# A vision block with a mixture of experts: tokens routed tile by tile during the attention, their scatters held back to half 57, five shared products moved to the end

## The chip, the cores and the metric

The kernel runs on one core of a Trainium2 chip. The metric is the device time in microseconds (us), as a median of several runs. A profiled execution gives the rows shown below; times in it count from its first instruction. The engines are PE (TensorE), DVE (VectorE), ACT (ScalarE), POOL (GpSimd) and SP (SyncE); each works through its own instruction list in order, and semaphores tie the lists together.

## What is computed

The input x is 32 images of 3 x 112 x 112. Each is cut into 49 patches of 16 x 16, so there are 1,568 tokens of width 256. All is float32.

```python
h = patches @ W.T + b                                   # embedding
h = h + attention(layernorm(h))                         # 16 heads, causal, a difference of two softmaxes, RMS norm per head
n = layernorm(h)
gates = softmax(n @ Wg.T)                               # 16 experts
scores, inds = top_k(gates, 2); scores /= sum(scores)
y = sum over the two chosen e of score_e * (silu(n @ Wgate_e.T) * (n @ Wup_e.T)) @ Wdown_e.T      # hidden 128
shared = (silu(n @ Sgate.T) * (n @ Sup.T)) @ Sdown.T                                              # hidden 512
out = h + y + sigmoid(n @ Wsg.T) * shared
```

## The kernel before, in words

Tokens are worked on in 16 tiles of 98 (two images). Every engine's list is written out by hand from the same numbered steps. After the embedding come the **halves**: `slot(u)` on each engine holds what that engine does at half u. Halves 0 to 63 are half an image of attention each (8 heads' scores on PE, row maximum and subtraction on DVE, exponential on ACT, weighing on PE); a tile's later steps follow at fixed distances (`tile_at(u, lag)` says which tile has its step of that lag at u). For tile t POOL normalises the heads (`normalise`, `difference`, `squares`, `head_norm` at half 4t+9), takes the inverse root of the second layer norm (`h2_inverse_root`, 4t+14; it gives `rs2`) and the low part of the normalised tokens (`h2_low`, 4t+19); DVE writes the normalised tokens to `hn2x` (4t+15); PE transposes them, and multiplies by the gate weights; DVE finds the two best experts (`top2`, 4t+23). So the last tiles drain through halves 64 to 83. POOL also makes `wsh_l`, the low part of the shared expert's weights, at halves 54 to 64.

Float32 products are run as three products of split values (a high and a low part): ACT makes the high part, DVE or POOL the low one.

The **shared expert** has 16 steps v of "up" work, each with a gate and an up product on PE (`shared_product`), a silu on ACT, the product on DVE (`shared_hidden`) and the split (`shared_high` on ACT, `shared_low` on DVE). Of each four steps four token tiles can be finished: `shared_down(t)` on PE, and a DVE instruction of the same name that adds `sig * product` to h (semaphore `sh_acc`). PE's `shared_down(t)` waits for `sh_acc` to reach t-1, that is for tile t-2 to be added, as two banks alternate. Steps 0 to 4 stand in the drain; steps 5 to 15, all the downs, and the splitting of the expert weights (`split_expert`) come behind the routing.

The **routing** of all tiles stands behind the drain. DVE makes one-hot rows, PE counts with two triangular products, DVE scans them and works out for each token and choice the row of `slots_x`, a buffer in HBM that is ordered by expert and padded to blocks of 128 rows (40 blocks). POOL then issues 32 indirect DMAs (`slots_x`, line 620: 16 tiles for the first choice, then, after all have landed and a column of token numbers was rewritten, 16 for the second). The buffer has been filled with padding rows by eight DMAs on POOL during the attention (`pad_rows`).

When the scatters have landed and all shared up products are done, SP loads block after block (`bx`), and the **experts** run: PE transposes, gate and up, transpose, down; POOL scatters results to `picked`. At the **end**, pieces of `picked` are loaded (`yt`) and added with their weights by DVE, and by ACT and POOL.

## Time and profile before

| | us |
|---|---|
| median of 3 runs (419.13, 424.42, 424.2) | 424.2 |
| the profiled execution's own time | 418.47 |
| its span, first to last instruction | 416.5 |
| PE busy in the span | 350.7 (84%) |
| POOL busy | 253.7 (61%) |
| DVE busy | 272.6 (65%) |
| ACT busy | 217.3 (52%) |

The span is 2 us short of its own execution's time. A busy share is a mean over stages which have different limits, so the rows below are read stage by stage. In rows of the chain and of the timeline, the first number is the start and the second the duration, in us; "L620" is line 620 of the kernel; a bracket says how long the engine stood idle before the instruction, and what ended that.

### The profile page before, as it was taken

Reading aid. Unit: us, or ns where it says so; the run is one execution under the profiler, and the core shown is the slowest. Engines: PE = TensorE matmul, PEld = TensorE weight load, DVE = VectorE, ACT = ScalarE, POOL = GpSimd, SP = SyncE. Lnnn points to the kernel's source line nnn. Section 1 sums busy time; section 2 is a strip of 40 time slices with the busy share of each in tenths; the row PEclk is TensorE's granted clock in tenths of the full one; section 3 lists DMA queues with packets and bytes.
Section 4 is the critical chain, followed back from the end, with each engine's and each line's share of the span. In section 5 each row is a group of like instructions: output and inputs, shape, how many; then the busy total and the mean of one; then the engine's idle time right before and its main releaser. Section 6 shows DMA issues by size and latency. Waiting matters only on the chain.

```text
span 416.5 us, 10603 instructions
## 1 busy us (share of the span) xinstructions
PE 350.7 (84%) x3418; PEld 317.5 (76%) x3419; DVE 272.6 (65%) x666; ACT 217.3 (52%) x554; POOL 253.7 (61%) x432
## 2 busy tenths in 40 slices
PE   3969998999999999999989877869996988899200
PEld 3869997888888888888878777869985987789100
DVE  4588446466766667678788747966762666676275
ACT  4424435567677777777677735224431554454040
POOL 5666745046566665676567871677772466777462
PEclk9989999899999999999999999969998899999755
DMA  7622664566364545664400000983125344541194
GB/s 253 192 57 82 139 134 103 66 116 108 78 98 116 108 97 64 120 111 133 140 2 2 2 1 2 354 303 102 52 78 153 98 135 128 153 130 54 40 302 122
DMA packets 33345, 47.18 MB, mean 113 GB/s; under 512 B 4538, under 2 KB 26750, under 8 KB 32528
## 3 DMA queue, kind: packets, MB, share of 16 engines
q1 hardware_dynamic: 24670, 29.12, 29.9%
q0 software_dynamic: 4864, 11.71, 8.6%
q10 hardware_dynamic: 3762, 5.72, 4.7%
q8 instruction: 28, 0.46, 0.4%
q14 instruction: 21, 0.17, 0.2%
HBM read 23.59 MB, written 15.34 MB: 93 GB/s over the span
## 4 chain that ended last, share of the span: by engine, by line
POOL 35%; issue 23%; PE 21%; DVE 11%; DMA 6%; ACT 2%; SPq 1%; POOLq 0%; DVEq 0%
PE bank L1162 9%; POOL slots_x L620 8%; POOL on L525 4%; PE bank L1393 3%; POOL att L533 3%; DMA xr<-xt 3%; POOL x_l L494 2%; PE bank L1357 2%; POOL rs L502 2%; POOL wsh_l L596 2%; POOL ao L556 2%; PE pair L1256 2%; POOL parts L507 2%; POOL picked L640 2%; DMA yt<-picked 1%
## 5 line engine op out<-in xcount | busy, mean ns | idle before, releaser
L1256 PE MATMUL pair<-vx,PT 113*113 113x128 f32 x512 | 68.2, 276 | 1.5 <-ACT raw L764 1.5
L1256 PEld LDWEIGHTS pair<-vx,PT 113*113 113x113 f32 x512 | 60.4, 177 | 2.7 <-issue 2.0
L969 DVE TENSOR_REDUCE smax<-bank 128x8 f32<-128x392 f32 x64 | 36.0, 563 | 38.1 <-PE bank L1235 38.0
L525 POOL TENSOR_TENSOR on<-raw,rz 128x256 f32<-128x256 f32 x32 | 19.9, 621 | 60.1 <-DVE rz L1027 60.1
L640 POOL DMA_INDIRECT picked<-by,bid x40 | 39.4, 984 | 24.3 <-DVE by L1140 14.6
L1245 PE MATMUL bank<-cs,Sm 114*113 114x114 f32 x256 | 41.6, 285 | 4.9 <-DVE Sm L977 4.8
L771 ACT ACTIVATE PT<-bank 113x456 f32<-113x456 f32 x64 | 35.2, 550 | 14.3 <-PE bank L1245 13.1
L620 POOL DMA_INDIRECT slots_x<-hn2x,slot_u x32 | 33.6, 1050 | 11.9 <-issue 9.1
L1245 PEld LDWEIGHTS bank<-cs,Sm 114*113 114x113 f32 x256 | 30.2, 177 | 8.2 <-DVE Sm L977 6.3
L977 DVE TENSOR_TENSOR Sm<-bank,smax 128x392 f32<-128x392 f32 x64 | 35.8, 559 | 0.5
L1174 PE MATMUL bank<-wt_h,x_h 128*98 128x256 f32 x96 | 29.0, 302 | 7.2 <-DVE wt_l L888 6.5
L764 ACT ACTIVATE raw<-pair 64x272 f32<-64x272 f32 x64 | 24.9, 390 | 11.2 <-PE pair L1256 10.4
L838 ACT ACTIVATE bxT_h<-bank 128x256 fp32r<-128x256 f32 x40 | 15.4, 384 | 29.3 <-PE bank L1357 28.8
L1235 PEld LDWEIGHTS bank<-Ks,Qs 48*49 48x49 bf16 x1024 | 18.2, 99 | 15.9 <-issue 15.9
L1174 PE MATMUL bank<-wt_h,x_l 128*98 128x256 f32 x96 | 28.4, 296 | 0.0
L1174 PE MATMUL bank<-wt_l,x_h 128*98 128x256 f32 x96 | 28.4, 296 | 0.0
L494 POOL TENSOR_TENSOR x_l<-xr,x_h 128x588 fp32r<-128x588 f32 x16 | 23.2, 1448 | 8.1 <-ACT x_h L668 7.6
L1128 DVE TENSOR_TENSOR bxT_l<-bank,bxT_h 128x256 fp32r<-128x256 f32 x40 | 17.0, 425 | 16.2 <-ACT bxT_h L838 13.8
L1162 PE MATMUL bank<-we_h,bxT_h 128*128 x80 | 26.9, 336 | 0.0
L1235 PE MATMUL bank<-Ks,Qs 48*49 48x49 bf16 x1024 | 25.0, 185 | 0.0
L749 ACT ACTIVATE hs_h<-hs 128x392 fp32r<-128x392 f32 x16 | 8.5, 532 | 31.3 <-DVE hs L985 28.6
L1162 PE MATMUL bank<-hn2T_h,wsh_h 128*128 128x392 f32 x64 | 23.2, 362 | 1.1 <-ACT sgl L743 1.1
(188 smaller groups left out, 1111.6 us busy)
## 6 DMA issues: line engine op xcount, KB each, us to landing
slots_x<-pad POOLq DMA_DIRECT2D x8, 642.5 KB, 7.5
bx<-slots_x SPq DMA_DIRECT2D x40, 128.5 KB, 2.1
Qs<-parts SPq DMA_DIRECT2D x48, 98.0 KB
Ks<-parts SPq DMA_DIRECT2D x48, 98.0 KB
we_raw<-we SPq DMA_DIRECT2D x4, 1024.0 KB, 7.9
xr<-xt ACTq DMA_DIRECT2D x13, 294.0 KB, 3.2
we_d<-we SPq DMA_DIRECT2D x1, 2048.0 KB, 8.9
yt<-picked SPq DMA_DIRECT2D x10, 196.0 KB
```

The costliest lines, as they stand in the source:

```text
L494: G.tensor_tensor(x_l[i % 3][:], xr[i % 3][:], x_h[i % 3][:].bitcast(F32), ALU.subtract).then_inc(x_lo, 1)
L525: G.tensor_tensor(on[:].rearrange("p b m d -> p (b m) d"), raw[b][:].rearrange("p b m n -> p (b m) n")[:, :, 0:16], bc(rz[b][:].rearrange( ...
L620: G.indirect_dma_start(out=slots_x, out_offset=bass.IndirectOffsetOnAxis(ap=slot_u[:, k, i:i + 1], axis=0), in_=hn2x[:, i, :], in_offset=N ...
L640: G.indirect_dma_start(out=picked, out_offset=bass.IndirectOffsetOnAxis(ap=bid[q][:], axis=0), in_=by[q][:], in_offset=None, bounds_check= ...
L771: A.activation(PT[b][:].rearrange("p a t -> p (a t)"), bank[2 + b][0:JT, 0:4 * IC], ACT.Exp).then_inc(exped, 1)
L969: V.tensor_reduce(smax[u % 2][:], score_of(u), AX.X, ALU.max).then_inc(maxed, 1)
L977: V.tensor_tensor(Sm[b][:].rearrange("p m j s -> p (m j) s")[:, :, 0:S], score_of(u), bc(smax[b][:].unsqueeze(2), [128, 8, S]), ALU.subtra ...
L1162: last = T.matmul(out, a, b, start=(3 * m + q == 0), stop=(3 * m + q == n - 1))
L1174: last = T.matmul(bank[6 + b][0:TT, 0:D], lhs, rhs, start=(k == 0 and q == 0), stop=(k == KP - 1 and q == 2))
L1235: last = T.matmul(bank[b][SLOT * jj:SLOT * jj + S, m * S:(m + 1) * S], Qs[g % 2][r, q, n * S:(n + 1) * S], Ks[g % 2][r, q, n * S:(n + 1) * ...
L1245: last = T.transpose(bank[2 + b][0:JT, m * IC:(m + 1) * IC], Sm[b][0:IC, m].rearrange("p j s -> p (j s)")[:, 0:JT], ident[0:IC, 0:IC])
L1256: last = T.matmul(bank[4 + b][0:JT, m * 2 * VN:(m + 1) * 2 * VN].rearrange("p (j n) -> p j n", j=2), PT[b][:, m, 0:JT], vx[i % NVX][:, :, ...
```

## The change

- **Regions in place of a packed order.** `slots_x` gets one region of 1,568 + 128 rows (REG) for each expert, so a token's row is the expert's base plus the number of earlier tokens there (`run`). This is known tile by tile: DVE does `top2` at half 4t+22, `one_hot` at 4t+23, `places` at 4t+25, `slot_rows` at 4t+26; PE counts the tile with two small products at 4t+23, and ACT copies the counts at 4t+24. The packed computation behind the drain is gone; a shorter one there finds for each of the 40 blocks its row and its expert.
- **Scatters** are issued by POOL within the halves, in pairs. Tile t's first choice goes at half 57+2t, its second two halves later, in front of the next tile's first; the second waits until the first of its tile has landed, as a column is rewritten in between. `ez` (for `sig`) moves from behind the drain into POOL's half 82, `ed` (for w1, w2) into half 86, behind the scatters of these halves. The halves now go up to 89.
- **Padding**: the eight DMAs on POOL go. SP writes 128 padding rows behind each region's end when the counts are known (17 DMAs, with row numbers read from registers), and loads blocks by row numbers from registers.
- **Shared expert**: up steps 5 to 7 and downs 0 to 2 go into halves 80 to 88; behind them only steps 8 to 15 and downs 3 to 10 are left before the experts, with the splits of expert weights beginning at step 9 (before, 7), and the last one behind step 15. Downs 11 to 15 stand behind the experts (BESIDE = 11), on PE and on DVE.

The constants:

```diff
+REG = TOK + BLK
+SPARE = E * REG
-        DRAINED = 5
-        FIRST_SPLIT = 7
+        DRAINED = 8
+        FIRST_SPLIT = 9
+        BESIDE = 11
-        LAST = 4 * (NT - 1) + 24
+        LAST = 4 * (NT - 1) + 30
+        def first_at(t):
+            return 57 + 2 * t
+        FIRST_AT = {first_at(t): t for t in range(NT)}
+        SECOND_AT = {first_at(t) + 2: t for t in range(NT)}
+        DOWN_AT = {86: 0, 87: 1, 88: 2}
```

SP, behind the loads of the expert weights (`we_raw`):

```diff
+            sp.dma_start(slots_x[SPARE:SPARE + BLK, :], pad[:]).then_inc(padded, 16)
+            sp.wait_ge(prow_known, 1)
+            for e in range(E):
+                if e % BX == 0:
+                    rows_of(prow, e, 0, SPARE - BLK)
+                sp.dma_start(slots_x[bass.ds(at[e % BX], BLK), :], pad[:]).then_inc(padded, 16)
             sp.wait_ge(eids_known, 3)
             sp.wait_ge(weights_known, 2)
+            sp.wait_ge(rows_known, 1)
             sp.dma_start(we_d[:], we[:, EGU:]).then_inc(wd_in, 16)
             sp.wait_ge(sh_u, NU)
```

POOL:

```diff
+            def scatter(k, t):
+                pool.wait_ge(slot_known, t + 1)
+                pool.wait_ge(hn2_done, t + 1)
+                if k == 1:
+                    pool.wait_ge(scattered[0], 16 * (t + 1))
+                    G.tensor_copy(hn2x[:].bitcast(U32)[:, t:t + 1, D], ids[:, 1, t:t + 1]).then_inc(ids_moved, 1)
+                    pool.wait_ge(ids_moved, t + 1)
+                G.indirect_dma_start(out=slots_x, out_offset=bass.IndirectOffsetOnAxis(ap=slot_u[:, k, t:t + 1], axis=0),
+                                     in_=hn2x[:, t, :], in_offset=None).then_inc(scattered[k], 16)
...
             def slot(u):
...
+                if u in SECOND_AT:
+                    scatter(1, SECOND_AT[u])
+                if u in FIRST_AT:
+                    scatter(0, FIRST_AT[u])
+                if u == 82:
+                    pool.wait_ge(logit_done, NT)
+                    G.tensor_tensor(ez[:], inverse_euler[:], logits[:, :, E], ALU.pow).then_inc(e_exp, 1)
+                if u == 86:
+                    pool.wait_ge(gate_diff, 1)
+                    G.tensor_tensor(ed[:], euler[:], dl[:], ALU.pow).then_inc(e_exp, 1)
                 if 54 <= u < 54 + 2 * NS and u % 2 == 0:
```

ACT, in `slot(u)`:

```diff
+                if (t := tile_at(u, 24)) is not None:
+                    act.wait_ge(counted, t + 1)
+                    act.wait_ge(run_done, t + 1)
+                    A.activation(ahead[:].rearrange("p a e -> p (a e)"), bank[7][0:TT, E + 1:3 * E + 1], ACT.Copy).then_inc(counts_kept, 1)
```

DVE, with its steps of `slot(u)` (`one_hot` stands first in a half, `places` and `slot_rows` near its end):

```diff
+            def one_hot(t):
+                dve.wait_ge(topped, 2 * t + 2)
+                V.tensor_copy(ixf[:], ix8[:, t, 0:TOPK]).then_inc(place_step, 1)
+                dve.wait_ge(place_step, 5 * t + 1)
+                V.tensor_tensor(oh[:], bc(iota.unsqueeze(1), [TT, TOPK, E]), bc(ixf[:].unsqueeze(2), [TT, TOPK, E]), ALU.is_equal).then_inc(place_step, 1)
+                dve.wait_ge(place_step, 5 * t + 2)
+                need(dve, counted, t)
+                V.tensor_tensor(both[:], oh[:, 0], oh[:, 1], ALU.add).then_inc(both_done, 1)
+
+            def places(t):
+                dve.wait_ge(counts_kept, t + 1)
+                dve.wait_ge(run_done, t + 1)
+                V.tensor_tensor(place[:], ahead[:, 0], run[:], ALU.add).then_inc(place_step, 1)
+                dve.wait_ge(place_step, 5 * t + 3)
+                V.tensor_tensor(chosen_at[:], oh[:], bc(place[:].unsqueeze(1), [TT, TOPK, E]), ALU.mult).then_inc(place_step, 1)
+
+            def slot_rows(t):
+                V.tensor_tensor(run[:], ahead[:, 1], run[:], ALU.add).then_inc(run_done, 1)
+                dve.wait_ge(place_step, 5 * t + 4)
+                V.tensor_reduce(slotr[:], chosen_at[:], AX.X, ALU.add).then_inc(place_step, 1)
+                dve.wait_ge(place_step, 5 * t + 5)
+                V.tensor_copy(slot_u[:, :, t], slotr[:]).then_inc(slot_known, 1)
...
+                if u == 86:
+                    dve.wait_ge(e_exp, 1)
+                    V.tensor_scalar(ez1[:], ez[:], 1.0, None, ALU.add).then_inc(routing, 1)
+                    dve.wait_ge(routing, 1)
+                    V.reciprocal(sig[:], ez1[:]).then_inc(weights_known, 1)
+                    dve.wait_ge(weights_known, 1)
+                if u - 1 in DOWN_AT:
+                    shared_down(DOWN_AT[u - 1])
```

DVE, behind the halves and still ahead of step 8 (this wait was there before, too, ahead of step 6):

```diff
             dve.wait_ge(e_exp, 2)
             link(V.tensor_scalar(ed1[:], ed[:], 1.0, None, ALU.add))
```

PE, in `slot(u)`, then in its table of up steps, then behind the experts:

```diff
+                if u in DOWN_AT:
+                    shared_down(DOWN_AT[u])
...
+            SHARED_AT = {66: (0, 0), 67: (0, 1), 69: (1, 0), 70: (1, 1), 71: (2, 0), 72: (2, 1), 73: (3, 0), 75: (3, 1), 76: (4, 0), 79: (4, 1),
+                         80: (5, 0), 81: (5, 1), 82: (6, 0), 83: (6, 1), 84: (7, 0), 85: (7, 1)}
...
+            pe.wait_ge(b_hT, NBLK)
+            for t in range(BESIDE, NT):
+                shared_down(t)
```

## Rows read from the trace of the kernel before

**Rows 1.** The chain that ended last, from the second scatters to the experts
```profile
293.64 0.96 POOL slots_x L620
...
314.07 2.53 DMA slots_x<-hn2x,slot_u
...
316.66 2.04 DMA bx<-slots_x
...
318.84 1.21 PE bank L1357 x4
```

**Rows 2.** Timeline of PE: a down's first product, an up step's, the next down's
```profile
302.97 0.28 PE L1162 MATMUL pair<-wsh_h,hs_h 128*98 128x256 f32 x1
...
304.38 0.34 PE L1162 MATMUL bank<-hn2T_h,wsh_h 128*128 128x392 f32 x1
...
306.55 0.28 PE L1162 MATMUL pair<-wsh_h,hs_h 128*98 128x256 f32 x1
```

**Rows 3.** Busy time by stretch: start:end length, PE, PEld, DVE, ACT, POOL, granted clock, DMA
```profile
220.99:250.12 29.13, 24.72 (x269) 21.46 (x267) 19.05 (x51) 18.26 (x47) 23.14 (x50) 1.00 0.01 2
...
100.00:200.00 100.00, 96.82 (x1273) 84.46 (x1272) 71.39 (x190) 70.66 (x181) 63.87 (x136) 1.00 0.55 110
270.00:280.00 10.00, 6.85 (x31) 6.56 (x30) 7.36 (x20) 2.77 (x5) 7.56 (x9) 0.72 0.91 314
```

**Rows 4.** Timeline of DVE: the tokens' write at half 39, a small routing step
```profile
176.53 0.75 DVE L1016 TENSOR_SCALAR hn2x<-h,mv,rs 98x256 f32<-98x256 f32 x1 [1.04 <-POOL rs L564]
...
264.26 0.17 DVE L1071 TENSOR_SCALAR cnts<-cnt 98x16 int32<-98x16 int32 x1
```

**Rows 5.** Timeline of POOL: its five waits in halves 57 to 71
```profile
223.06 0.62 POOL L525 TENSOR_TENSOR on<-raw,rz 128x256 f32<-128x256 f32 x1 [0.26 <-DVE rz L1027]
...
228.75 0.62 POOL L525 TENSOR_TENSOR on<-raw,rz 128x256 f32<-128x256 f32 x1 [1.29 <-DVE rz L1027]
...
233.15 0.62 POOL L525 TENSOR_TENSOR on<-raw,rz 128x256 f32<-128x256 f32 x1 [0.25 <-DVE rz L1027]
...
238.41 0.62 POOL L525 TENSOR_TENSOR on<-raw,rz 128x256 f32<-128x256 f32 x1 [0.92 <-DVE rz L1027]
...
247.00 0.21 POOL L546 TENSOR_TENSOR nt<-r 128x16 f32<-128x16 f32 x1 [1.31 <-ACT r L786]
```

**Rows 6.** The scatters by line: nanoseconds of one; landing, all and those at 262-275
```profile
L620 POOL DMA_INDIRECT slots_x<-hn2x,slot_u x32: 942/949/1965, 269.2 to 314.1; - x32
...
DMA to landing us min/median/max: 2.5/2.7/8.0
...
DMA to landing us min/median/max: 3.1/4.0/8.0
```

**Rows 7.** Timeline of POOL: a power of 98x16, a one-column copy of token numbers
```profile
260.94 2.91 POOL L608 TENSOR_TENSOR ed<-euler,dl 98x16 f32<-98x16 f32 x1 [0.55 <-DVE dl L1057]
...
318.83 0.18 POOL L629 COPY bid<-bx 128x1 uint32<-128x1 uint32 x1 [3.82 <-DMA bx<-slots_x]
```

**Rows 8.** Timeline of PE: a down after a wait, and the next down
```profile
275.26 0.50 PE L1162 MATMUL pair<-wsh_h,hs_h 128*98 128x256 f32 x1 [3.15 <-DVE h L1115]
...
281.59 0.28 PE L1162 MATMUL pair<-wsh_h,hs_h 128*98 128x256 f32 x1
```

**Rows 9.** Timeline of DVE: a split of expert weights, and two steps' shared hidden
```profile
284.77 1.23 DVE L1107 TENSOR_TENSOR we_l<-we_raw,we_h 128x1024 fp32r<-128x1024 f32 x1 [0.38 <-ACT we_h L826]
...
304.50 0.56 DVE L985 TENSOR_TENSOR hs<-sgl,bank 128x392 f32<-128x392 f32 x1
...
308.14 0.55 DVE L985 TENSOR_TENSOR hs<-sgl,bank 128x392 f32<-128x392 f32 x1
```

**Rows 10.** Timeline of POOL: the scatter issued beside that split
```profile
284.87 1.95 POOL L620 DMA_INDIRECT slots_x<-hn2x,slot_u  x1 [0.30 <-issue]
```

**Rows 11.** Timeline of PE's last instruction, and of DVE's first addition of results
```profile
387.56 1.22 PE L1393 MATMUL bank<-we_d,bhT 128*128 x4
...
397.25 0.49 DVE L1150 SCALAR_TENSOR_TENSOR h<-yt,w,h 98x256 f32<-98x256 f32 x1 [8.00 <-DMA yt<-picked]
```

More of the change, by code:

```diff
@@ L141, in build @@
         woff = keep("woff", [1, NBLK // BX + 1, 2 * BX], I32)
+        pad = keep("pad", [128, ROW])
+        ixf = keep("ixf", [TT, TOPK])
+        oh = keep("oh", [TT, TOPK, E], BF16)
+        both = keep("both", [TT, E], BF16)
+        ahead = keep("ahead", [TT, 2, E])
+        place = keep("place", [TT, E])
+        chosen_at = keep("chosen_at", [TT, TOPK, E])
+        slotr = keep("slotr", [TT, TOPK])
+        run = keep("run", [TT, E])
+        prow = keep("prow", [1, E], I32)
+        rows = keep("rows", [1, NBLK], I32)
         one_bf = keep("one_bf", [128, 128], BF16)
@@ L234, in build @@
         hs_l = [la(f"hs_l{n}", [128, SB, SH], F32R) for n in range(2)]
+        ya = Zone(late.at, ceiling).take
         we_h = la("we_h", [128, EGU], F32R)
@@ L270, in build @@
         bid = [ba(f"bid{n}", [BLK, 1], U32) for n in range(BX)]
-        ya = Zone(shared.at, ceiling).take
         yt = [ya(f"yt{n}", [TT, TOPK, YG, D]) for n in range(NT // YG)]
@@ L445, in _, with rows_of @@
                 sp.dma_start(we_raw[:, cols], we[:, cols]).then_inc(we_in[n], 16)
+            regs = [SP.alloc_register(f"row{n}") for n in range(BX)]
+            at = [None] * BX
+            def rows_of(table, n0, low, high):
+                SP.load(regs, table[0:1, n0:n0 + BX])
+                for n in range(BX):
+                    at[n] = SP.snap(regs[n], min_val=low, max_val=high)
             def load_block(b):
+                if b % BX == 0:
+                    rows_of(rows, b, 0, SPARE)
                 if b >= BX:
@@ L1047, in _ @@
                 slot(u)
-            dve.wait_ge(topped, 2 * NT)
-            done = [0]
+            done = [1]
             def link(ins):
@@ L1064, in _ @@
[L1064 to L1070 removed]
+            dve.wait_ge(run_done, NT + 1)
@@ L1272, in slot @@
                     need(pe, logit_done, t)
+                    need(pe, counts_kept, t - 1)
                     for k in range(KD):
@@ L1287, in slot @@
                     end.then_inc(gated, 1)
+                if (t := tile_at(u, 23)) is not None:
+                    pe.wait_ge(both_done, t + 1)
+                    pe.wait_ge(logit_done, t + 1)
+                    T.matmul(bank[7][0:TT, E + 1:2 * E + 1], up_bf[0:TT, 0:TT], both[:], start=True, stop=True)
+                    T.matmul(bank[7][0:TT, 2 * E + 1:3 * E + 1], one_bf[0:TT, 0:TT], both[:], start=True, stop=True).then_inc(counted, 1)
                 if 0 <= u - 2 < HALVES:
@@ L1336, in shared_down @@
                                                      for b in range(SB)]).then_inc(sh_y, 1)
-            for v in range(DRAINED, NU + DOWN_LAG):
-                if v < NU:
-                    shared_product(v, 0)
-                    shared_product(v, 1)
+            for i in range(NT + 1):
+                step(i)
+            slot(0)
+            for i in range(NT + 1, NT + 4):
+                step(i)
+            for u in range(1, LAST):
+                slot(u)
+            for v in range(DRAINED, NU):
+                shared_product(v, 0)
+                shared_product(v, 1)
                 shared_down(v - DOWN_LAG)
```

227 lines of the change are left out of this document (93 added, 134 removed).

## The prediction

> **What bounds the kernel now.** I read the chain first. From the last scatters it runs straight into the experts: the last indirect DMA starts at 314.07 and lands 2.53 later, a block is loaded in 2.04, and the experts' first product starts at 318.84 [rows 1]. The reader is to see that scatters pace this stretch: from 293.64 to 314.07 fifteen steps take 20.4, so 1.36 each. But they are not alone. PE's timeline [rows 2] shows the shared expert beside them: a down takes 1.41 (302.97 to 304.38), an up step 2.17 (304.38 to 306.55). Step 15 ends at 306.55, and six downs more carry PE nearly to the landing of the scatters. So two paths end within a microsecond of each other, and a change has to shorten both. In the attention PE is busy 96.8 of 100 us [rows 3]: it sets the pace there. Last I read POOL from half 57 on, since the change puts its scatters there: between 220.99 (start of half 57) and 250.12 (end of half 71) its waits are only 0.26, 1.29, 0.25, 0.92 and 1.31 [rows 5]. It has 4.03 us to spare in 29.13, so 25.1 of its own work (23.1 by busy time alone [rows 3]; the rest is gaps between dependent steps). That is the finding on which the forecast rests.
>
> **Ahead of half 57.** Nine tiles are routed: eight small DVE instructions each, at 0.17 [rows 4] and some gap, say 1.6 us; two small PE products, one ACT copy. Most of the DVE work falls into waits like the 1.04 ahead of the tokens' write [rows 4]; what doesn't, and PE's own two products, I take as 0.2 to 0.25 a tile, an estimate, since PE has only 3.2% to spare: 2 us, with 0 (all hidden) and 4 (a quarter of DVE's 1.6 x 9 = 14.4) as ends. POOL's eight padding DMAs go, which gives nothing where PE sets the pace. So half 57 starts on POOL at 223.0.
>
> **POOL from half 57 to half 71.** Added are first scatters of tiles 0 to 7 and second ones of 0 to 6: 15 x 1.36 = 20.4. Seven copies of token numbers at 0.18 [rows 7] with a gap make 1.8. Their landing waits are hidden by other work here. 25.1 + 20.4 + 1.8 = 47.3, against 29.1 before: POOL ends half 71 at 270.3 instead of 250.1. This doesn't stay on POOL. DVE's write of the normalised tokens waits for POOL's root and stands ahead of the subtraction that PE's transposes need, so the last attention halves are held too; and `wsh_l` in half 64, which PE's first shared product needs, comes some 9 us later. The ends: 23.1 of own work and the median of 0.95 [rows 6] with a gap of 0.3 take off 2.0 and 1.7.
>
> At one place a rule of the Trainium skill can be weighed. A scatter that began at 284.87, a tenth after a DVE split of two SBUF operands at 284.77, took 1.95 instead of 0.95 [rows 9, 10]. The Trainium skill (SBUF — State Buffer, section "SBUF: two separate sides") says that DVE and GpSimd share a port pair under an exclusive lock, and that GpSimd cannot write a DMA's descriptors while DVE holds it; the trace agrees at this place. By the rule, were each of the 25 scatters up to `ez` held by 1.0 as this one was, the sum would be 25 higher, beyond the last rival below. The 1.36 used here is a mean that holds such cases as often as they came.
>
> **From half 73 on** POOL has little else to do, and the pair itself is a chain: the second scatter of a tile waits for the landing of its first. Landing 2.53, copy 0.2, gap 0.3, and the second's pitch of 1.3 make 4.3 a tile. Tile 7's first starts at about 269.0, tile 11's therefore at 286.2. In half 74 lies the last root, near 274.5, and in half 79 the last `h2_low`, near 283; what is left of POOL's own work fits into the landing waits. `h2_low` releases the loads of the expert weights, so the next landing competes with 4 MB: I take 4.0, the median of the five beside those loads, not 2.53; the ends are 2.5 and 8.0 [rows 6]. Tile 12's first then starts at 292.0 and ends at 293.0, and `ez`, moved behind it, ends 2.9 later [rows 7]: 295.9.
>
> **What waits for `ez`.** DVE stands in half 86 at `sig`; queued behind it are the hidden product of step 7 and the down of tile 0. PE has by then done steps 0 to 7 and downs 0 and 1 (tile 15's gate product comes near 277; behind it are seven single products of half of 2.17 and two downs, 10.4, and some waits: about 289) and stands at down 2, which needs the down of tile 0 on DVE. Two small DVE steps, the hidden product and the down (0.25 + 0.2 + 0.55 + 0.5) put PE's start at 297.4. Left on PE up to the end of step 15 are eight downs, 11.3, and eight up steps, 17.4: 326.1. After the only such wait before (3.15) the granted clock of that stretch was 0.72, a mixture of 1.2 and 2.4 GHz, and a down and an up step took 6.33 (275.26 to 281.59) instead of 3.58 [rows 2, 3, 8]; here PE idles for 8, so I add 2.8 (ends 0 and 2.8): step 15 ends at 328.9, against 306.55.
>
> `ed`, behind the pair of half 85, ends near 307; DVE waits for it ahead of the hidden product of step 8, which PE needs for the up half of step 10, at about the same time. I cost that at 0, with 2 as upper end.
>
> **From step 15 to the experts.** Of the six downs that stood here one is left, so the five moved ones give 7.0. But the splits now begin two steps later and the last stands behind step 15. DVE starts a step's hidden product 1.6 after PE ended it (308.14 against 306.55), its round takes 3.64, and the last split 1.23 more [rows 2, 9]: the experts, which need all splits, start 6.5 after step 15, at 335.4, against 318.84. That is +16.6. Scatters don't end last: after `ed` two tiles are left, landed near 316. The padding on SP, 17 small DMAs, stands in front of the load of the down weights, but that load waits for `ed` as well; it has from 307 to PE's 328.9 to land.
>
> **The experts and the end.** Per block nothing changes; row numbers in registers are read eight at a time, ahead of loads with eight blocks' lead: 0, or up to 2. Downs 11 to 15 take 7.0 on PE after 388.78, and DVE's part 0.6, while the first results arrive 8.5 after PE's end [rows 11]: 0. If PE ran them at the lower clock they would take twice that, and the end would be 5 later.
>
> **Sum.** 418.47 + 16.6 = 435.1 on the profiled execution's footing, of which attention is 2.0, landing beside the loads 1.5, and the clock 2.8. The profiled time lies with the lowest of the three runs, 5.7 under their median; on the median's footing it is 440.8. I name 437, between them. With all low ends (2.0, 2.0, 1.7, 1.5, 2.8) 6.6 is left, with the high ones (2 + 4 + 2 + 2 + 5 more) about 32.
>
> **Rivals.**
> - *POOL has room after all (faster).* If gaps and landings cost nothing, POOL's time to `ez` is 23.1, 2 more of late own work, 25 x 0.95 = 23.8 and 2.9, from 220.99: 272.8. Then PE is released at 274.3, ends step 15 at 303.0, and the experts start at 309.5: 9.3 less, 409 to 415. It gains where `ez` ends before 282. For it: the landing lies beside other work in most halves. Against it: the scatters stood 1.36 apart where POOL did nothing else, not 0.95 [rows 1, 6], and the landing is awaited by name. Chance 0.06.
> - *The same sum with the low ends (no difference that can be measured, about 2% here).* Attention hides the routing, the landings stay at 2.5, the clock holds: +3 to +8.5, 422 to 433. For it: almost no transfers in halves 57 to 71 (2 GB/s) [rows 3]. Against it: all ends would have to fall low. Chance 0.22.
> - *The forecast*, +9 to +20: 427 to 444. Chance 0.58.
> - *Landings of 8 beside the loads, for two or three tiles*, so that `ed` too holds DVE and PE, or downs at the end that show: +21 to +32, 440 to 455. The 8.0 speaks for it, the median of 2.7 against it [rows 6]. Chance 0.14.
>
> The change may also fail of its aim at one point only, the moved downs, if they lengthen the end: that is the 5 in the high ends. Eight in ten: I leave out the gain and most of the last case, 424 to 446. Faster by over 2%: 0.06; within: 0.22; slower: 0.72.
>
> **What the profile after would show.** POOL without waits between halves 57 and 71, ending there near 270; landing as what ends POOL's waits from half 73 on; `ez` near 296; PE idle for several us ahead of down 2, released by DVE's h; step 15 ending near 329, the experts starting 6 to 7 later, behind a DVE split and not behind a block's load; the end unchanged. I am wrong if scatters beside the attention are shorter than 0.95, if POOL still waits in halves 57 to 66, or if PE's down 2 doesn't wait.

## The result, and the profile after

Slower, by more than the range allowed: 457.79 us as a median of four runs (451.95 to 462.99), against 421.66 for the kernel before on the same chip; ratio 1.077, 95% interval 1.058 to 1.097. Forecast were 437.0 and 424 to 446. Medians in this document are over all runs of a kernel, while ratios and intervals compare only the executions without the slower state that both kernels sometimes fall into (for the changed kernel 451.95 and 456.51). The profiled execution of the changed kernel is its slowest run (462.99; span 461.1; mean granted clock 0.902, for the kernel before 0.944), so its rows say more about places than about the median. Two more profiles of the unaltered kernel, below, repeat what is read here.

The chain that ended last, in order of time (start, duration, what); it answers to [rows 1]:

```profile
360.31 0.96 ACT we_h L862
361.27 0.02 issue
361.29 1.23 DVE we_l L1167
362.52 0.39 DVE h L1031
362.91 1.14 DVE we_l L1167
364.05 0.04 issue
364.10 0.70 PE bank L1414 x2
```

Not a scatter and not a block's load leads into the experts now, but the splits of the expert weights, as forecast. The experts start at 364.10 instead of 318.84: 45.3 later.

POOL's timeline: half 57's first row, the last row of half 71, then the rows up to `ed` ([rows 5, 7]):

```profile
245.97 0.22 POOL L580 TENSOR_TENSOR nt<-r 128x16 f32<-128x16 f32 x1
...
292.36 0.95 POOL L613 DMA_INDIRECT slots_x<-hn2x,slot_u  x1 [0.30 <-issue]
...
311.26 0.96 POOL L613 DMA_INDIRECT slots_x<-hn2x,slot_u  x1 [0.30 <-issue]
317.31 0.18 POOL L611 COPY hn2x<-ids 98x1 uint32<-98x1 uint32 x1 [5.10 <-DMA slots_x<-hn2x,slot_u]
...
320.31 2.96 POOL L636 TENSOR_TENSOR ez<-inverse_euler,logits 98x16 f32<-98x16 f32 x1
...
331.03 3.55 POOL L639 TENSOR_TENSOR ed<-euler,dl 98x16 f32<-98x16 f32 x1
```

From 245.97 to 293.31 halves 57 to 71 take 47.3, the very sum that was forecast. But they begin at 245.97, 25.0 later than before, where 2 were forecast. Behind them `ez` ends 30.0 later (forecast 25.6); POOL's longest wait for a landing on the way is 5.10, behind the first scatter of tile 11 (311.26).

The scatters by line ([rows 6]), and `both`, the sum of the two one-hot rows (ns, least, median, most), each as the view of its line or tile gives it:

```profile
L613 POOL DMA_INDIRECT slots_x<-hn2x,slot_u x32: 952/973/1802, 248.2 to 343.4; - x32
...
DMA to landing us min/median/max: 2.5/2.6/6.3
```

```profile
L1052 DVE TENSOR_TENSOR both<-oh x16: 166/978/2282, 135.8 to 306.8; 98x16 bf16<-98x16 bf16 x16
```

DVE's timeline in the attention, `ez`, the hidden products of steps 8 and 15, the last down, and the first result ([rows 4, 9, 11]):

```profile
179.55 1.08 DVE L1052 TENSOR_TENSOR both<-oh 98x16 bf16<-98x16 bf16 x1
180.56 0.55 DVE L1006 TENSOR_REDUCE smax<-bank 128x8 f32<-128x392 f32 x1
...
323.31 0.17 DVE L1118 TENSOR_SCALAR ez<-ez 98x16 f32<-98x16 f32 x1 [9.19 <-POOL ez L636]
...
335.32 0.56 DVE L1022 TENSOR_TENSOR hs<-sgl,bank 128x392 f32<-128x392 f32 x1
...
359.19 0.55 DVE L1022 TENSOR_TENSOR hs<-sgl,bank 128x392 f32<-128x392 f32 x1
...
440.98 0.48 DVE L1031 SCALAR_TENSOR_TENSOR h<-pair,sig,h 98x256 f32<-98x256 f32 x1 [0.92 <-PE pair L1217]
443.53 0.48 DVE L1205 SCALAR_TENSOR_TENSOR h<-yt,w,h 98x256 f32<-98x256 f32 x1 [2.08 <-DMA yt<-picked]
```

PE's timeline at half 22, at a counting product, at down 2, at the first product of down 10 (it follows step 15), and at the experts ([rows 2, 8]):

```profile
136.59 2.05 PE L1311 MATMUL pair<-vx,PT 113*113 113x128 f32 x8 [2.70 <-issue]
...
180.69 0.21 PE L1347 MATMUL bank<-both,up_bf 98*98 98x16 bf16 x1 [1.24 <-DVE both L1052]
...
324.91 0.50 PE L1217 MATMUL pair<-wsh_h,hs_h 128*98 128x256 f32 x1 [7.93 <-DVE h L1031]
...
355.80 0.32 PE L1217 MATMUL pair<-wsh_h,hs_h 128*98 128x256 f32 x1
...
364.10 1.11 PE L1414 MATMUL bank<-cs,bx 128*128 128x128 f32 x4 [6.68 <-DVE we_l L1167]
```

Three rows speak of the attention. `both` adds 16 numbers per partition and takes 1.08, and 2.28 at most, where the small step of before took 0.17 [rows 4]; PE's counting product waits 1.24 for it; and once, at half 22, PE stands 2.70 with nothing to wait for that the profile shows. The other rows were forecast: the wait for `ez` (7.93; forecast 8) and the splits that release the experts. PE stands 6.68 for these, but only behind down 10; from the end of step 15 (355.80, where down 10 starts) to the experts it is 8.3, where 6.5 were forecast. The moved downs are over on DVE at 441.46, before the first result at 443.53: they are hidden.

By stretch, in attention (start:end length, PE, PEld, DVE, ACT, POOL, granted clock, DMA), as [rows 3]:

```profile
151.00:163.00 12.00, 10.75 (x116) 9.48 (x115) 9.04 (x27) 6.90 (x20) 6.31 (x14) 0.86 0.35 39
163.00:175.00 12.00, 10.77 (x140) 9.40 (x139) 9.76 (x30) 7.86 (x22) 5.61 (x13) 1.00 0.34 44
```

PE's busy time falls from 96.8% to just under 90%, and in the first of the two its granted clock is 0.86, a mixture of 1.2 and 2.4 GHz, where before it was 1.00 throughout [rows 3].

So from profile to profile (spans 416.5 and 461.1): 25.0 ahead of half 57, 18.2 in halves 57 to 71 (forecast 18.2), 2.1 from there to the experts (forecast 3.6 less), 0.7 less behind them. Of the 25.0, 3.8 are there at half 1 already (its row maximum at 80.76 instead of 76.93); other kernels of the new form have 75.20 to 85.07 there, so that part is not shown to be the change's.

### The profile page after: what moved, and what is told of

Same layout as the page of the kernel before. It is cut to its first block, busy times and chain, and to the rows that moved or that the text cites. A ratio compares the mean times of both kernels' runs of the same rounds, so it can differ in the third digit from the quotient of the medians.

```text
span 461.1 us, 11109 instructions
## 1 busy us (share of the span) xinstructions
PE 373.6 (81%) x3448; PEld 338.0 (73%) x3449; DVE 299.2 (65%) x788; ACT 219.3 (48%) x570; POOL 250.1 (54%) x439
## 4 chain that ended last, share of the span: by engine, by line
PE 31%; issue 18%; POOL 17%; DVE 14%; DMA 10%; SPq 6%; ACT 2%; POOLq 0%; DVEq 0%; ACTq 0%
PE bank L1217 10%; PE pair L1311 7%; SPq L447 5%; DMA slots_x<-hn2x,slot_u 4%; PE bank L1300 4%; PE bank L1450 3%; POOL slots_x L613 3%; PE bank L1290 3%; DMA xr<-xt 2%; PE bank L1414 2%; DMA Ks<-parts 2%; POOL wsh_l L644 2%; DVE both L1052 2%; DMA yt<-picked 2%; ACT we_h L862 2%
## 5 line engine op out<-in xcount | busy, mean ns | idle before, releaser
L1311 PE MATMUL pair<-vx,PT 113*113 113x128 f32 x512 | 74.8, 293 | 3.0 <-issue 2.7
L1311 PEld LDWEIGHTS pair<-vx,PT 113*113 113x113 f32 x512 | 66.5, 193 | 4.4 <-issue 3.3
L671 POOL DMA_INDIRECT picked<-by,bid x40 | 39.2, 981 | 26.6 <-DVE by L1193 16.9
L1300 PE MATMUL bank<-cs,Sm 114*113 114x114 f32 x256 | 44.5, 300 | 2.6 <-DVE Sm L1014 2.6
L1300 PEld LDWEIGHTS bank<-cs,Sm 114*113 114x113 f32 x256 | 32.4, 189 | 5.2 <-DVE Sm L1014 3.0
L1290 PEld LDWEIGHTS bank<-Ks,Qs 48*49 48x49 bf16 x1024 | 19.2, 103 | 17.1 <-issue 17.1
L1217 PE MATMUL bank<-hn2T_h,wsh_h 128*128 128x392 f32 x64 | 25.3, 396 | 3.0 <-POOL wsh_l L644 2.5
L1414 PE MATMUL bank<-cs,bx 128*128 128x128 f32 x80 | 16.6, 294 | 12.3 <-DVE we_l L1167 6.7
L1290 PE MATMUL bank<-Ks,Qs 48*49 48x49 bf16 x1024 | 26.1, 188 | 0.0
```

Source lines behind the costliest of these rows:

```text
L671: G.indirect_dma_start(out=picked, out_offset=bass.IndirectOffsetOnAxis(ap=bid[q][:], axis=0), in_=by[q][:], in_offset=None, bounds_check= ...
L1217: last = T.matmul(out, a, b, start=(3 * m + q == 0), stop=(3 * m + q == n - 1))
L1290: last = T.matmul(bank[b][SLOT * jj:SLOT * jj + S, m * S:(m + 1) * S], Qs[g % 2][r, q, n * S:(n + 1) * S], Ks[g % 2][r, q, n * S:(n + 1) * ...
L1300: last = T.transpose(bank[2 + b][0:JT, m * IC:(m + 1) * IC], Sm[b][0:IC, m].rearrange("p j s -> p (j s)")[:, 0:JT], ident[0:IC, 0:IC])
L1311: last = T.matmul(bank[4 + b][0:JT, m * 2 * VN:(m + 1) * 2 * VN].rearrange("p (j n) -> p j n", j=2), PT[b][:, m, 0:JT], vx[i % NVX][:, :, ...
L1414: last = T.transpose(bank[par][:, k * BLK:(k + 1) * BLK], bx[q][:, k * 128:(k + 1) * 128], ident)
```

## The experiments

My theory after reading the trace: the routing beside the attention costs what came in ahead of half 57, most of it by `both`, which POOL's work holds up on DVE. The rival: it is something else of the new program (the embedding, its code, the scatters and their landings). Each expectation says what either would give.

For every profile I read three stage lengths from DVE's row maxima and PE's first expert product. They say where a change of the time lies. Each is from one execution, so the clock of that execution is in it:

| kernel | median us (runs) | half 22 to 26 | half 26 to 57 | half 57 to experts |
|---|---|---|---|---|
| before | 420.5 to 424.9 (four medians) | 10.88 | 79.52 | 99.16 |
| changed | 457.79 (4) | 17.62 | 95.29 | 118.01 |
| again | 458.70 (4) | 16.61 | 92.89 | 119.21 |
| both_reduced | 445.20 (4) | 17.55 | 82.77 | 119.24 |
| counts_late | 452.49 (4) | 16.27 | 88.22 | 118.97 |
| scatters_behind | 459.79 (4) | 17.51 | 95.80 | 119.30 |
| late_routing | 442.32 (4) | 16.21 | 78.69 | 120.15 |
| spread | 440.87 (4) | 18.08 | 96.05 | 99.19 |
| ez_early | 459.44 (4) | 17.96 | 95.49 | 119.92 |
| spread_all | 430.66 (4) | 16.54 | 85.58 | 101.21 |
| pads | 457.32 (4) | 10.90 | 94.33 | 119.42 |
| downs_ahead | 460.34 (4) | 18.15 | 92.86 | 124.63 |
| best | 419.08 (5) | 14.73 | 88.39 | 94.61 |
| best_pads | 427.29 (4) | 10.90 | 90.26 | 92.24 |
| pads_2 | 456.24 (6) | 10.90 | 98.16 | 118.31 |
| again_2 | 457.07 (6) | 13.30 | 92.90 | 119.13 |
| ez_ed_early | 446.93 (6) | 16.61 | 95.69 | 108.00 |
| best_second | 414.09 (6) | 12.40 | 82.30 | 91.41 |

Runs of one kernel lie up to 15 apart here, so a difference of 2 between two medians says nothing.

### The attention ahead of half 57

**again** is the changed kernel, unaltered. 

> The changed kernel once more, unaltered, for a second profile. In the first one half 57 starts on POOL at 245.97 instead of 220.99, 25 later, where 2 was forecast; 3.8 of it stand already at half 1, and 6.7 come between halves 22 and 26, around one stall of PE of 2.70 for which nothing is shown. Theory A (the routing steps beside the attention hold DVE and PE, some 1.2 to 2.1 a tile): about 15 to 18 of the 25 come again, the 3.8 and the 6.7 may not. Theory C (the profiled execution was disturbed as a whole): under 8 come again. Time by A 450 to 458, by C under 445.

 Measured 458.70, just above theory A's range. POOL's half 57 starts at 242.88, so 21.9 of the 25 come again: 3.7 of them are there at half 1 (80.61), and the stall of 2.70 at half 22 is there too. Theory C fell.

**both_reduced** takes the sum from one operand:

```diff
-                V.tensor_tensor(both[:], oh[:, 0], oh[:, 1], ALU.add).then_inc(both_done, 1)
+                with nc.allow_low_precision(reason="zeros and ones"):
+                    V.tensor_reduce(both[:], oh[:].rearrange("p k e -> p e k"), AX.X, ALU.add).then_inc(both_done, 1)
```

> One DVE instruction altered: the sum of the two one-hot rows is a reduction over one operand instead of an addition of two. Theory A (that addition of two SBUF operands is held by POOL's instruction, 1.08 instead of 0.17, and PE stands 1.24 behind it in front of its counts): the instruction falls to 0.2, PE's wait to under 0.5, and the time by 0.8 x 10 tiles, some 8 us, against the changed kernel. Theory B (it is the number of DVE's instructions in front of the row maximum that delays, not the hold): the time falls by under 2 us. Also possible under A: the hold moves to the next instruction of two operands, then under 4 us.

 Measured 445.20, 12.6 less than the changed kernel's first median and 13.5 less than again. The same tile's view:

```profile
L1053 DVE TENSOR_REDUCE both<-oh x16: 185/186/189, 131.9 to 290.5; 98x16 bf16<-98x32 bf16 x16
```

0.19 each time, and half 26 to 57 falls by 10.1 against again. Some of the 10.1 is PE's clock: it was granted 1.00 there and 0.96 in again. So most of the routing's price in that stage is one instruction of 16 elements per partition, with what it does to the clock. How it comes to 1.08 can be read from POOL beside it, in the changed kernel:

```profile
179.42 0.55 POOL L598 TENSOR_TENSOR rs<-ve,half_neg 98x1 f32<-98x1 f32 x1
179.94 0.61 POOL L575 TENSOR_TENSOR sq<-att 128x256 f32<-128x256 f32 x1
180.51 0.56 POOL L603 TENSOR_TENSOR hn2T_l<-h2T,hn2T_h 128x196 fp32r<-128x196 f32 x1
```

`both`, with two operands in SBUF, is listed from 179.55 to 180.63 and ends 0.08 behind POOL's `sq` (180.55); in each of the eight tiles from 154 to 238 of this trace it ends 0.06 to 0.09 behind `sq`. Near the end, where nothing of POOL's or only a scatter lies beside it, it takes 0.17. With one operand it takes 0.19 beside the same work. The row maximum of the half, which PE needs, stands behind it. The Trainium skill (SBUF — State Buffer, section "SBUF: two separate sides") has this as an exclusive lock between a DVE operation on two SBUF operands and a GpSimd operation that reads SBUF, for a whole instruction. The two forms, 1.08 and 0.19, agree with it; but the trace shows `both` held over two instructions of POOL's, the end of `rs` and all of `sq`, and over three where it takes 2.28. In the kernel before it was the tokens' write that ended behind POOL's `sq` (0.75 [rows 4]; 0.96 as a mean of nine from 135 to 235). In the changed kernel it starts later and takes 0.40, as `both` has taken the wait.

**counts_late** puts PE's two count products behind the weighing of their half:

```diff
+                if 0 <= u - 2 < HALVES:
+                    weigh(u - 2)
                 if (t := tile_at(u, 23)) is not None:
                     pe.wait_ge(both_done, t + 1)
...
-                if 0 <= u - 2 < HALVES:
-                    weigh(u - 2)
```

> PE's two count products stand behind the weighing of the same half instead of ahead of it; DVE is left as it is. Theory A: PE's wait of 1.24 a tile is covered by the 1.05 of the weighing, 5 to 10 us less than the changed kernel, in the attention alone. Theory B (DVE's row maximum and subtraction come late, and the next half's transposes wait for them): PE's wait only moves to the transposes, 0 to 3 us less.

 Measured 452.49, 6 less than again; half 26 to 57 falls by 4.7. That is theory A, at the low end of its range. What a wait costs is thus also a matter of what is queued behind it.

**late_routing** routes only tiles 9 to 15: each `tile_at` at lags 23 to 26 becomes `routed`, and the semaphores count from tile 9. It leaves out the expert results of tiles 0 to 8.

```diff
+        N0 = 9
+
+        def routed(u, lag):
+
+            t = tile_at(u, lag)
+            return t if t is not None and t >= N0 else None
```

> This kernel leaves out the routing of tiles 0 to 8 (one-hot rows, counts, places): their tokens go to fixed rows that no block reads, and the last additions take other tiles' results; scatters keep their number and places. Theory A (the routing beside the attention is what came in ahead of half 57): POOL's half 57 begins near 222 to 228 in place of 242 to 246, the stall of 2.4 to 2.7 on PE at half 23 is gone or stands at half 59 now, where the first count products are, and the time is 434 to 442. Rival B (something else of the new program slows the attention, such as the embedding or the layout of its code): half 57 begins at 236 or later, and the time stays above 450.

 Measured 442.32, at the upper end of theory A's range; POOL's half 57 starts at 225.33 (222 to 228 expected). Half 26 to 57 takes 78.69, as before (79.52): so all of the 13 to 16 there is the routing. The theory stands, with one exception:

```profile
132.62 2.05 PE L1319 MATMUL pair<-vx,PT 113*113 113x128 f32 x8 [2.42 <-issue]
```

The stall at half 22 is still there, with no tile routed yet. There the theory fell.

**pads** and **pads_2** put the eight padding DMAs of before back on POOL, into a buffer that nobody reads:

```diff
+                if u % 6 == 5 and u // 6 < NT // 2:
+                    pad_rows(u // 6)
```

> The changed kernel with the eight padding DMAs of the kernel before put back on POOL at their old halves, into a buffer that nothing reads; nothing else differs. Theory C (PE stands 2.4 to 2.7 at half 22 in every kernel of the new form, with the routing of tiles 0 to 8 or without it, because its instructions arrive later when the padding DMAs don't lie beside the stacking loads; 5.5 to 6.7 with the low clock behind it): the stall is gone, half 22 to half 26 takes 10.9 again, and the time is 451 to 454. Rival (the stall is due to something else, as where the code lies): it stays at 2.4 to 2.7, and eight DMA instructions of 0.83 on POOL leave the time at 457 to 462.

 Measured 457.32. The stall is gone in all three runs with these DMAs (pads, pads_2, best_pads): half 22 to 26 takes 10.90 in each. It is there, 1.62 to 2.70, in each of the fourteen other profiles of the new form. Queues in one microsecond (packets, MB, share), first late_routing from 129 to 130, then the kernel before from 126 to 127:

```profile
q1 hardware_dynamic: 84, 0.06, 51.7%
q8 instruction: 1, 0.02, 10.3%
```

```profile
q0 software_dynamic: 30, 0.10, 26.4%
q1 hardware_dynamic: 81, 0.06, 19.3%
q8 instruction: 1, 0.02, 6.3%
```

A packet of instructions (16 KB, the ninth of 28 in queue q8) starts 2.9 ahead of half 22 in the kernel before (row maximum at 129.28), and only 0.1 ahead of it in late_routing (129.48); PE stands from 130.2 to 132.6. The same holds in every profile: with the padding DMAs the ninth packet starts 2.2 to 2.9 ahead of half 22, without them from 1.4 ahead to 0.1 behind, and PE then stands ahead of the same product each time and goes on 1.5 to 1.8 after the packet has ended. Where it came 1.4 ahead (best_second), the stall is the shortest, 1.62. So PE's stall follows the arrival of this packet. The padding DMAs (q0), which the diff removes and which I costed at nothing, lay beside the loads that stack queries and keys (q1). That the packet holds PE's instructions is likely, as 6,897 of the 11,109 instructions are PE's products and weight loads; how the padding brings it forward is argued and not shown. That the stall comes and goes with those DMAs is shown.

Its price is less clear, so pads_2 ran beside **again_2**, the unaltered kernel. 

> The changed kernel with the eight padding DMAs beside the attention again, in more rounds and beside the unaltered kernel on the same chip. In its first run the stall at half 22 was gone, yet the medians lay only 1 apart. If the stall costs what the two traces differ by from half 22 to half 26 (16.6 to 18 against 10.9), less eight DMA instructions that POOL has room for: 4 to 7 faster than the unaltered kernel of this call. Rival (the time is given back later, as POOL paces from half 57 on): 0 to 2.

 

> The changed kernel, unaltered, in more rounds, for the run beside it: 455 to 461, and PE stands 2.4 to 2.7 at half 22 once more.

 Measured 456.24 and 457.07: 0.8 apart, the rival (and 457.32 for pads, where its theory had 451 to 454). In the profile of pads_2 half 26 to 57 takes 98.16, in that of again_2 92.90. The stretches show why, pads_2 first:

```profile
146.00:158.00 12.00, 10.76 (x115) 9.35 (x113) 8.92 (x28) 6.85 (x19) 6.67 (x15) 0.86 0.34 38
```

```profile
145.00:157.00 12.00, 10.75 (x140) 9.37 (x139) 9.92 (x30) 7.86 (x22) 6.31 (x14) 1.00 0.35 40
```

With the same wait of 1.24 per tile, the granted clock is 0.86 in one execution and 1.00 in the other; four halves take 13.44 in the one and 12.06 in the other (before: 10.88 at 1.00). This hides what the stall costs. Within half 22 to 26 the clock decides it as well: at 1.00 the four halves take 12.40 and 13.30 (best_second, again_2), which is the stall alone on top of 10.88; at 0.71 to 0.79 they take 16.2 to 18.2. So the stall's price in the median stays open.

### From half 57 to the experts

**scatters_behind** keeps the routing and issues all 32 scatters behind the halves. 

> The routing stays in the attention, but all 32 scatters stand behind the last half, first all first choices, then all second ones, as before the change. Theory of the prediction (scatters fill POOL from half 57 on and hold ez, and ez holds PE): half 57 starts as late as in the changed kernel; halves 57 to 71 take about 29 on POOL instead of 47; ez ends soon after the last tile's logits, PE doesn't wait for it; scatters take 32 x 1.36 = 44 behind the halves, so they and the shared downs end close together again, and the experts start some 20 to 25 earlier than in the changed kernel: 430 to 438, still 10 to 18 above the kernel before. Rival (the scatters beside the attention cost little, the loss is the routing's alone): no earlier than 5 us below the changed kernel.

 Measured 459.79, a miss: half 57 to the experts takes as long, because the scatters now end last. `ez` is early, as expected (302.73, and PE doesn't wait for it). But halves 57 to 71 take 35.6 on POOL without any scatter, not 29, as the routing beside them holds the other engines, and the 32 scatters take 54.6 from 310.78 on, not 44.

```profile
370.17 1.19 PE L1413 MATMUL bank<-cs,bx 128*128 128x128 f32 x4 [28.43 <-DMA bx<-slots_x]
```

**spread** issues them earlier instead:

```diff
-            return 57 + 2 * t
+            return 4 * t + 27
```

> One size changed: tile t's first scatter is issued at half 4t+27, right behind its rows, in place of 57+2t. Theory A (in the drain POOL's own list paces, and fifteen scatters of 1.36 lengthen it): from half 57 on DVE to tile 13's low part takes 33 to 37 in place of 43; ahead of half 57 POOL has 3.3 more to do per 10.9 of a tile, which with a busy share of 64% costs 0 to 8 in sum; ez ends before 305 and PE's wait ahead of down 2 is gone; time 440 to 452. Rival (a scatter costs the same wherever it stands, since it holds POOL and DVE against each other): half 57 begins 10 to 15 later than in the changed kernel, and the time stays at 455 to 462.

 Measured 440.87. Half 57 to the experts takes 99.19, as before the change, 18.8 less than in the changed kernel; half 26 to 57 takes 96.05 against 92.89 to 95.29. On POOL halves 57 to 71 take 38.2 in place of 47.3, `ez` ends 19.4 behind them in place of 30.0, and PE doesn't stand ahead of down 2. PE's granted clock in the stage is 0.94 and not 0.86, so some of the 18.8 is the clock that came back with the shorter waits. So holding the scatters back to half 57 is what costs in this stage.

**ez_early** moves `ez` from half 82 to half 80. 

> ez stands two halves earlier on POOL (half 80, ahead of tile 11's second and tile 12's first scatter). Theory A (PE's wait of 7.9 ahead of down 2 is the wait for ez): that wait falls to 2 to 4, the experts start 3 to 5 earlier, time 453 to 456. Rival (ed, or another row of POOL's chain of landings, holds PE instead): PE stands as long at a later place, and the time stays within 2 of 458.7.

 Measured 459.44: nothing, and PE's wait moved:

```profile
312.67 0.33 PE L1217 MATMUL pair<-wsh_h,hs_h 128*98 128x256 f32 x1 [1.59 <-DVE h L1031]
...
333.46 0.69 PE L1217 MATMUL bank<-hn2T_h,wsh_h 128*128 128x392 f32 x1 [10.98 <-DVE hs L1022]
```

The expected 3 to 5 fell, the rival held: `ed`, which DVE awaits ahead of step 8, holds PE longer than `ez` did (10.98, and 7.93 in the changed kernel). **ez_ed_early** moves both:

```diff
-                if u == 82:
+                if u == 80:
                     pool.wait_ge(logit_done, NT)
...
-                if u == 86:
+                if u == 82:
                     pool.wait_ge(gate_diff, 1)
...
-                if u == 84:
+                if u == 83:
                     dve.wait_ge(topped, 2 * NT)
```

> ez at half 80 and ed at half 82, both ahead of tile 13's first scatter (ez alone gave nothing: PE then stood 10.98 for step 8's hidden product, which stands behind ed on DVE). Theory: the two powers, and what POOL's chain of landings puts ahead of them, are the path from the end of the attention to step 8; PE's waits of 9.4 and 0.3 shrink to under 4, the experts start 6 to 9 earlier and the time is 449 to 453. Rival: scatters of tiles 13 to 15 come 3 to 6 later and hold the experts by their landing: then 455 to 459.

 Measured 446.93, about 10 less than again_2, 11.1 in this stage: more than the 6 to 9 expected. The rival (late scatters hold the experts) didn't come.

**downs_ahead** sets BESIDE to 16. 

> The changed kernel with all downs ahead of the experts (BESIDE = 16), as before the change. If the five moved downs are worth what they cost on PE (5 x 1.41) and are hidden behind the experts: experts 5 to 7 later (the last splits then have cover and take back 1 to 2), time 463 to 466. Rival: the splits behind step 15 cover them, and the time stays at 457 to 461.

 Measured 460.34. In the trace the experts come 5.4 later from half 57 on than in again, as the theory had it; the medians (460.34, 458.70) lie within their spread, so a gain of the moved downs in the time is not shown.

### Towards a better version

**spread_all** is spread with both_reduced and counts_late. 

> Three edits in one: scatters right behind their rows (half 4t+27), the sum of the two one-hot rows as a reduction over one operand, and the count products behind the weighing of their half. If the three causes add up: 445.2 of the reduction alone, less 3 for the counts, less 5 to 12 for the scatters, so 430 to 437, still above the kernel before. Rival: the scatters in the attention fill POOL so that DVE and PE wait for it there; then 440 to 448, no better than the reduction alone.

 Measured 430.66, at the low end of the range. The gains add up in part: alone the three took 12.6, 5.3 and 16.9 off the 457.79, together 34.8, and here it is 27.1. The sum and the counting products both act on PE's wait for `both`.

**best** adds, in the drain:

```diff
-        FIRST_AT = {first_at(t): t for t in range(NT)}
-        SECOND_AT = {first_at(t) + 2: t for t in range(NT)}
+        FIRST_AT = {**{first_at(t): t for t in range(13)}, 85: 13, 86: 14, 87: 15}
+        SECOND_AT = {**{first_at(t) + 2: t for t in range(13)}, 86: 13, 87: 14, 89: 15}
-        FIRST_SPLIT = 9
+        FIRST_SPLIT = 8
...
                 shared_hidden(v)
+                split_expert(v - FIRST_SPLIT)
                 shared_low(v)
-                if 0 <= v - FIRST_SPLIT:
-                    split_expert(v - FIRST_SPLIT)
                 shared_down(v - DOWN_LAG)
-            split_expert(NG - 1)
```

Besides, `ez` stands at half 81, `ed` at 84 and `dl` at 83, all ahead of the last three tiles' scatters, and ACT makes the high part of a split ahead of the step's.

> The three edits together (scatters right behind their rows, the sum of the one-hot rows by a reduction, count products behind the weighing), and in the drain ez at half 81 and ed at 84, ahead of the scatters of tiles 13 to 15, and the splits of expert weights one step earlier and between a step's hidden product and its low part. If ez, ed and the splits behind step 15 are what is left on the path: PE's wait ahead of down 2 of 2.7 goes, and the experts start 4 to 5 after step 15 and not 6.7; 430.7 less 3 to 7, so 424 to 428, within 1.5% of the kernel before. Rival: PE's own work is the path there; 429 to 431.

 Measured 419.08, ratio 0.990 (0.983 to 0.997): 11.6 less than spread_all, where 3 to 7 were expected, so it missed on the good side. Half 57 to the experts takes 94.61, 4.6 less than before the change. The edits of the drain weren't run apart, so which of them gave how much is open. **best_pads** adds the padding DMAs. 

> The previous kernel with the eight padding DMAs put back beside the attention, into a buffer that nothing reads. Theory C: 5 to 6 less than the previous kernel, 418 to 422, level with the kernel before. Rival: the stall at half 22 stays, and eight DMAs more on POOL leave it equal or 1 to 3 slower.

 Measured 427.29, ratio 1.012 (1.003 to 1.022): slower than best, though the stall is gone. It missed, and which of its waits does it is open. In the profile of best, its slowest run (431.01), a landing shows inside the attention, on POOL:

```profile
175.53 0.19 POOL L611 COPY hn2x<-ids 98x1 uint32<-98x1 uint32 x1 [4.53 <-DMA slots_x<-hn2x,slot_u]
```

DVE's write of tokens waits 4.36 behind it, PE 4.29. **best_second** gives the second scatter of tiles 0 to 12 four halves instead of two. 

> The best kernel so far with the second scatter of tiles 0 to 12 four halves behind the first, in place of two. In its trace POOL stood 4.5 once for the landing of a first scatter beside the stacking loads, and DVE and PE 4.4 and 4.3 behind it. If such waits still cost time: they are gone, and the time is 412 to 418 (ratio to the kernel before 0.98 to 0.99). Rival: they are rare, and the time stays at 418 to 421.

 Measured 414.09 (410.45 to 416.11), ratio 0.981, 95% interval 0.975 to 0.987: faster than the kernel before, by 1.3 to 2.5%. In its trace no copy of tiles 0 to 11 waits for a landing (tile 12's: 0.48), and half 26 to 57 takes 82.30.

## Why the prediction was wrong

**The step that failed is "Ahead of half 57".** It was sized at 2 us (0 to 4) and measured 21 in the changed kernel's profile, without the 3.8 of the embedding; in again_2 it is 16 (22 to 57 takes 106.20 against 90.40), of which 2.4 lie between halves 22 and 26 and 13.4 behind. Three things were in it. First, `both`: I took eight DVE instructions at 0.17, from a row of a step that stood where POOL was idle [rows 4]. Beside POOL's work ahead of half 57 `both` takes 0.31 once, then 0.88 to 2.28, and the rows of before had such a case in plain sight, the tokens' write with 0.75. I asked whether DVE has room (71.4 of 100 [rows 3]), not what stands behind the instruction: the half's row maximum, which paces PE. Made of one operand, the step gives back 10.1 of the 13.4 that half 26 to 57 takes longer in again, the clock's part included. Second, the clock: waits of 1.24 in each tile come with 0.86 in some stretches of some executions, 1.4 more for each tile there. Third, the padding DMAs "which gives nothing": without them PE stands at half 22 and the four halves take 1.5 to 7.3 longer in the traces. What that costs in the median is open.

**Halves 57 to 71** were right to the tenth (47.3), and by their terms: the fifteen scatters take 20.2 with the idle time ahead of each (20.4 in the sum), and POOL waits for other engines only 0.38 and 0.31. spread, with 38.2, shows that this is the cost of holding the scatters back. That half 71 then ended 23 later than forecast comes from the step above.

**From half 73 on** was short by 4.4: `ez` came 30.0 and not 25.6 behind half 71. Two terms were too small. A pair was to take 4.3 per tile and took 4.7 from tile 7 to tile 11 (292.36 to 311.26): between copy and scatter POOL mostly stands 0.56, where I had 0.3. And the landing beside the loads was to take 4.0; tile 11's took 5.9, so that POOL stood 5.10 for it. The rival with landings of 8 didn't come in this profile (6.3 is the longest); the two further profiles each have one above 8, but behind `ed`. The time, above that rival's range too, didn't come from there.

**What waits for `ez`** was right as a row (7.93 for 8) and incomplete as a cause: `ed`, costed at 0, holds PE even longer (10.98) when `ez` is out of the way. A wait costed at 0 because another one ends as late is no free wait.

**From step 15 to the experts** the cause was right (the last splits release them) and the size short: 8.3 for 6.5. I took it that DVE starts step 15's hidden product 1.6 after PE ended the step [rows 2, 9]; it started 3.4 after (359.19 against 355.80). DVE had stood for `ed` ahead of step 8, whose hidden product starts at 335.32, 4.5 behind that step, and a round of DVE with a split, 3.64, is no shorter than a down and an up step on PE, 3.58, so it didn't catch up. With `ed` earlier (ez_ed_early) the distance is 8.3 again; best, where DVE's rounds of that place take 2.5, has 3.3. The round and the last split behind step 15 came as taken. The moved downs were right (hidden, as the last rows of DVE show; 7.0 in the sum, 5.4 in the trace), and so was **the end** (0.7 less). The rival of a gain (POOL has room) fell with the 47.3.

Together: the forecast on the profiles' footing was 16.6. Add 23.0 ahead of half 57, 4.4 up to `ez` and 1.3 from there to the experts, less 0.7 at the end, and it is the 44.6 that was measured.

The rule that I weighed and put aside was the right one in the wrong place. I charged the lock to POOL's scatters. The traces bear out that a scatter can be held: those that start inside a DVE split of two operands end 0.8 behind it (1.95 [rows 10], 1.80 at most in the changed kernel), and one that starts 0.03 ahead of a split, at 288.37 in the kernel before, takes 0.95. What I drew there from the Trainium skill (SBUF — State Buffer, section "SBUF: two separate sides") on descriptors is told of DVE's two-port modes, which such a split doesn't have; what agrees is the exclusive lock. But few scatters meet a split (their median is 0.97), and the mean that I used held. The rows that the lock cost were DVE's, in the attention.

## What to carry to other kernels

Price an added instruction from a row with the same neighbours on the other engines, and look first at what stands behind it in its own list: `both`, with about 1 us for each tile ahead of the row that paces the attention, cost some 10 of the 13.4 there, while fifteen scatters put into the same part of POOL's list (spread) made half 26 to 57 at most 3.2 longer. A small step with two SBUF operands on DVE beside a busy POOL is worth rewriting with one operand (12.6 us here). Work that is held back to run in one piece meets the stretch where its engine's own chain sets the pace; spread over the time before, it took 17 us less, though the kernel was still 4.7% slower than the one it started from (ratio 1.047). Only with the one-operand sum, later counting products, earlier powers and splits, and room between a transfer and what awaits it, did it become 1.9% faster.

## What was not expected of the hardware

- An addition of 98 x 16 bf16 numbers took 0.17 alone and up to 2.28 beside POOL's work, held over up to three of POOL's instructions; as a reduction over one operand it took 0.19 each of 16 times.
- PE stood 1.62 to 2.70 at half 22, waiting for nothing that the profile shows, in every kernel without the padding DMAs (14 profiles), and in none of the four profiles with them, the kernel before among these. It went on 1.5 to 1.8 after a packet of instructions had ended. Removing DMAs can delay an engine that never waited for them.
- With equal waits of 1.24 per tile, PE's granted clock was 1.00 in one profile and 0.86 in another, of two kernels whose PE lists don't differ: 12.06 and 13.44 for four halves. In the changed kernel both occur in one execution.
